# A graph layer on one core: dense units moved from the last stage to the third hop, and standard deviations picked for eight tiles at once

## What is computed

```python
def _spmm(edge_src, edge_dst, edge_weight, feats, n_nodes):
    msgs = edge_weight[:, None] * feats[edge_src]
    return jax.ops.segment_sum(msgs, edge_dst, num_segments=n_nodes)
feats = [x]
cur = x
for _ in range(n_blocks - 1):
    cur = _spmm(edge_src, edge_dst, edge_weight, cur, n_nodes)
    feats.append(cur)
concat = jnp.concatenate(feats, axis=1)
return concat @ shared_weight + output_bias
# then: x = _layernorm(x + that, axis=-1)
```

## Time and profile before

| | us |
|---|---|
| median of three runs | 1876.14 |
| lowest, highest | 1869.22, 1887.84 |
| the profiled execution | 1871.29 |
| its span, first to last instruction | 1869.5 |

### The profile page before, as it was taken

The page is one execution under the profiler, slowest core; times in us unless marked ns, Lnnn a source line. Parts: engine busy times, 40 slices in busy tenths (PEclk is TensorE's granted clock), DMA queues, the critical chain, the costliest instruction groups (busy, mean ns, idle before and its releaser), DMA issues. The chain is left out here.

```text
span 1869.5 us, 31494 instructions
## 1 busy us (share of the span) xinstructions
PE 1526.1 (82%) x7964; PEld 1254.5 (67%) x7964; DVE 1193.9 (64%) x5229; ACT 1086.5 (58%) x2674; POOL 1068.6 (57%) x1047
## 2 busy tenths in 40 slices
PE   7889888888888877488889998878877777777884
PEld 5777777777777755367768887766666656666773
DVE  6766655555556566666644445878877777777564
ACT  4665666666666643256655554656665655556565
POOL 4566666566656653656646664456555555555554
PEclk9999999999999988699989999989998888888997
DMA  8888878878778879389877776878887777777563
GB/s 253 262 262 265 268 247 260 269 252 265 253 250 267 261 232 370 107 264 310 301 232 186 187 191 208 272 239 293 270 269 256 245 242 261 242 246 249 187 206 116
DMA packets 224954, 458.74 MB, mean 245 GB/s; under 512 B 30805, under 2 KB 133144, under 8 KB 224778
## 3 DMA queue, kind: packets, MB, share of 16 engines
q1 hardware_dynamic: 174326, 349.30, 56.3%
q0 software_dynamic: 49456, 106.72, 19.7%
q10 hardware_dynamic: 996, 0.72, 0.2%
HBM read 239.08 MB, written 226.07 MB: 249 GB/s over the span
## 5 line engine op out<-in xcount | busy, mean ns | idle before, releaser
L1362 PE MATMUL ps_y<-w_sb,xT 128*128 128x256 f32 x2640 | 739.2, 409 | 92.9 <-DVE y_ring L1680 67.2
L1362 PEld LDWEIGHTS ps_y<-w_sb,xT 128*128 128x128 f32 x2640 | 502.6, 205 | 165.2 <-issue 65.5
L1680 DVE TENSOR_TENSOR y_ring<-ps_y,bias 128x512 f32<-128x512 f32 x391 | 268.9, 688 | 330.0 <-remote 161.7
L1087 ACT ACTIVATE o_ring<-y_ring,shift,rstd 128x256 f32<-128x256 f32 (+1 forms) x782 | 422.3, 590 | 0.0
L1686 DVE BATCH_NORM_STATS2 stats<-y_ring 128x6 f32<-128x256 f32 (+1 forms) x782 | 291.3, 414 | 7.4 <-remote 2.0
L827 POOL DMA_INDIRECT tails_found<-tail_keys,table_idx x200 | 201.5, 1007 | 150.5 <-issue 60.2
L827 POOL DMA_INDIRECT rows_in<-out_rows,tailx_idx x160 | 163.0, 1018 | 211.9 <-DVE sums L2329 83.0
L827 POOL DMA_INDIRECT rows_in<-in_x,gather_idx x200 | 201.2, 1006 | 128.9 <-issue 70.7
L1074 ACT COPY xT<-ps_xT 128x512 f32<-128x512 f32 x268 | 154.2, 576 | 182.7 <-remote 122.8
L831 POOL DMA_INDIRECT out_rows<-u_out,tailo_idx x197 | 200.6, 1018 | 95.5 <-issue 54.9
L1351 PE MATMUL ps_xT<-ident,x_ring 128*128 128x128 f32 x1196 | 191.7, 285 | 29.3 <-ACT xT L1074 18.6
(11 more groups left out here) (279 smaller groups left out, 2380.9 us busy)
## 6 DMA issues: line engine op xcount, KB each, us to landing
x_ring<-in_x SPq DMA_DIRECT2D x195, 512.0 KB
out_rows<-o_ring SPq DMA_DIRECT2D x195, 512.0 KB
c_rows<-zeros SPq DMA_DIRECT2D x50, 512.0 KB
c_rows<-sums SPq DMA_DIRECT2D x49, 512.0 KB
u_rows<-u_out SPq DMA_DIRECT2D x49, 512.0 KB
keys_bc<-keys_out SPq DMA_DIRECT2D x64, 256.0 KB
keys_bc<-u_rows SPq DMA_DIRECT2D x25, 512.0 KB
tails_found<-u_rows SPq DMA_DIRECT2D x12, 512.0 KB
```

What stands on the lines that cost most here:

```text
L1087: last = act.activation(o_ring[slot][0:rows, r * D:(r + 1) * D], y_ring[k][0:rows, r * D:(r + 1) * D], ACT.Identity, bias=shift[k][0:rows, ...
L1362: last = pe.matmul(ps_y[p % 2][0:rows, r * D:(r + 1) * D], columns_of(p)[0][:, q * P:q * P + rows], w_sb[:, c, :], start=c == 0, stop=c == ...
L1680: dve.tensor_tensor(y_ring[k][0:rows, half * 2 * D:(half + 1) * 2 * D], ps_y[half][0:rows, :], bias2[0:rows, :], ALU.add).then_inc(y_copie ...
```

## The change

- The ten first groups of the third hop carry two dense units each, not one. SP gets one store and one load more in each.
- The twenty kept steps of the last stage carry four and three units by turns, not four each. So ten units move from the last stage to the third hop.
- The window of deviations is 14 units wide, not 16, beginning 4 units before the tile's place, not 5.
- The three bfloat16 parts are no longer made for each step. They cover all windows, and are made in four splits (units 0 to 96 before the last stage, then 28, 24 and 14 units in steps 7, 13 and 16), in memory of buffers that are free by then.
- The one-hot matrices of partitions are made in slots 2 and 3. Column marks for all eight tiles of a step are made in one instruction in slot 5 of the step before (`mark_cols`); in slot 0 one instruction multiplies them with the spread values, in slot 1 one sums (`pick_std`, `sum_picked`).

```diff
-    D_UNIT = C_UNIT + ONE * FIRST_GROUPS + FOUR
+    D_UNIT = C_UNIT + PAIR * FIRST_GROUPS + FOUR
-    WINDOW = 16
-    WINDOW_BACK = 5
+    WINDOW = 14
+    WINDOW_BACK = 4
-    D_SIZES = (FOUR,) * KEPT_STEPS + (STEP,) * (D_STEPS - KEPT_STEPS)
+    D_SIZES = (FOUR, STEP) * (KEPT_STEPS // 2) + (STEP,) * (D_STEPS - KEPT_STEPS)
+    SPLITS = ((0, 0, 96), (7, 96, 124), (13, 124, 148), (16, 148, kept_window(KEPT_STEPS - 1)[1]))
...
-    bridge_d = (D_UNIT - FOUR, FOUR, 0, ONE)
+    bridge_d = (D_UNIT - FOUR, FOUR, 0, PAIR)
     def c_step(g):
-        return C_UNIT + ONE * g, ONE, 0, ONE if g > 0 else STEP
+        return C_UNIT + PAIR * g, PAIR, 0, PAIR if g > 0 else STEP
...
                 store_behind(c_step(g), 0)
                 if g > 0:
                     load_own(G * g + 3, 3)
+                    load_ahead(c_step(g - 1), 1)
+                store_behind(c_step(g), 1)
...
             def spread_std(d, q):
                 if q == 0:
-                    pe.wait_ge(std_chain, 6 * d + 6)
-                    until(pe, std_picked, Q * (d - 1))
+                    pe.wait_ge(parts_hot, 2 * d + 2)
+                    pe.wait_ge(std_split, 1 + 4 * splits_before(max(d - 1, 0)))
+                    until(pe, std_picked, d - 1)
...
-            def prepare_std(d, q):
+            def split_std(s, part):
+                step, first, end = SPLITS[s]
+                cols = RPP * (end - first)
+                whole = std_all[:, RPP * first:RPP * end]
+                high, mid, low = (t[:, RPP * first:RPP * end] for t in std_parts)
+                rest = std_rest[:, 0:cols]
+                if part == 0:
+                    dve.tensor_copy(high, whole).then_inc(std_split, 1)
+                if part == 1:
+                    dve.wait_ge(std_split, 4 * s + 2)
+                    dve.tensor_tensor(rest, whole, high, ALU.subtract).then_inc(std_split, 1)
+                if part == 2:
+                    dve.wait_ge(std_split, 4 * s + 3)
+                    dve.tensor_copy(mid, rest).then_inc(std_split, 1)
+                if part == 3:
+                    dve.wait_ge(std_split, 4 * s + 4)
+                    dve.tensor_tensor(low, rest, mid, ALU.subtract).then_inc(std_split, 1)
+
+            def mark_cols(d):
+                first, end = kept_window(d)
+                cols = RPP * (end - first)
+                until(dve, std_picked, d)
+                dve.tensor_tensor(col_hot[:, :, 0:cols],
+                                  window_col[:, WCOLS - cols:WCOLS].unsqueeze(1).broadcast_to([P, Q, cols]),
+                                  tail_col[:, Q * d:Q * d + Q].unsqueeze(2).broadcast_to([P, Q, cols]),
+                                  ALU.is_equal).then_inc(cols_hot, 1)
-            def pick_std(n, q, d):
-                dve.scalar_tensor_tensor(out=picked_out[q][:, 0:cols], in0=window_col[:, WCOLS - cols:WCOLS], scalar=tail_col[:, n:n + 1],
-                                         in1=ps_std[d % 2][:, WCOLS * q:WCOLS * q + cols], op0=ALU.is_equal, op1=ALU.mult,
-                                         accum_out=row_std[d % 2][:, q:q + 1]).then_inc(std_picked, 1)
+            def pick_std(d):
+                first, end = kept_window(d)
+                dve.wait_ge(std_spread, Q * d + Q)
+                dve.wait_ge(cols_hot, d + 2)
+                dve.tensor_tensor(window_view(d, picked_out), window_view(d, ps_std[d % 2][:, 0:Q * WCOLS]),
+                                  col_hot[:, :, 0:RPP * (end - first)], ALU.mult).then_inc(std_picked, 1)
+            def sum_picked(d):
+                dve.wait_ge(std_picked, d + 1)
+                dve.reduce_sum(row_std[d % 2][:, :], window_view(d, picked_out), mybir.AxisListType.X).then_inc(std_found, 1)
...
             def c_restore(n, q, d, part, turn):
-                dve.wait_ge(std_picked, n + 1)
+                dve.wait_ge(std_found, d + 3)
...
-                    if n < KEPT:
-                        pick_std(n, q, d)
+                    if n < KEPT and q < 2:
+                        (pick_std, sum_picked)[q](d)
...
-                    if d + 1 < KEPT_STEPS and q < G:
-                        prepare_std(d + 1, q)
+                    for s in range(1, len(SPLITS)):
+                        if SPLITS[s][0] == d and q < 4:
+                            split_std(s, q)
+                    if d + 1 < KEPT_STEPS and q in (2, 3):
+                        mark_parts(d + 1, q - 2)
+                    if d + 1 < KEPT_STEPS and q == 5:
+                        mark_cols(d + 1)
```

More of the change, by code:

```diff
@@ L81, in kept_window, with splits_before @@
         return max(Q * d - WINDOW_BACK, 0), Q * d - WINDOW_BACK + WINDOW
+    SPLITS = ((0, 0, 96), (7, 96, 124), (13, 124, 148), (16, 148, kept_window(KEPT_STEPS - 1)[1]))
+    def splits_before(d):
+        return sum(step <= d for step, first, end in SPLITS)
+    assert all(end <= (D_OFFS[step] - STEP if step > 0 else D_UNIT - FOUR - STEP) for step, first, end in SPLITS)
+    assert all(kept_window(d)[1] <= SPLITS[splits_before(max(d - 1, 0)) - 1][2] for d in range(KEPT_STEPS))
+    assert max(end - first for step, first, end in SPLITS) * RPP * 4 <= Q * P * 2
+    SPLIT_COLS = RPP * kept_window(KEPT_STEPS - 1)[1]
+    assert 3 * SPLIT_COLS <= Q * SLOTS
     assert all(kept_window(d)[1] <= (D_OFFS[d - 1] if d > 0 else D_UNIT - FOUR) - STEP for d in range(KEPT_STEPS))
@@ L137, in gnn_program @@
         cT = [sb(f"cT{k}", [P, 2 * D]) for k in range(2)]
-        sel = [sb(f"sel{k}", [P, P]) for k in range(G)]
+        sels = sb("sels", [P, G, P])
+        sel = [sels[:, k, :] for k in range(G)]
         keys_bc = [sb(f"keys_bc{k}", [P, Q * P]) for k in range(2)]
@@ L708, in _ @@
                 group_c(g)
-            load_ahead(c_step(FIRST_GROUPS - 1), 0)
+            for k in range(PAIR):
+                load_ahead(c_step(FIRST_GROUPS - 1), k)
             with sp.Fori(FIRST_GROUPS, n_groups) as g:
@@ new lines, in mark_parts, with window_view @@
+            def mark_parts(d, half):
+                part = 2 * (d % 2) + half
+                until(dve, std_spread, Q * (d - 1) + G * half + G)
+                dve.wait_ge(node_parts_in[part], 16 * A_STEPS + 16 * (d // 2) + 16)
+                dve.tensor_scalar(part_hot[:, half * G * P:(half + 1) * G * P], node_part_bc[part], part_number[:, 0:1], None,
+                                  ALU.is_equal).then_inc(parts_hot, 1)
+            def window_view(d, table):
+                first, end = kept_window(d)
+                return table.rearrange("p (q c) -> p q c", c=WCOLS)[:, :, 0:RPP * (end - first)]
```

59 lines of the change are left out of this document (24 added, 35 removed).

## The result

| | us |
|---|---|
| before, 20 runs beside it, median | 1869.49 |
| after, 20 runs, median | 1877.43 |
| lowest, highest of after | 1865.24, 1887.73 |
| ratio after / before | 1.0053, 95% interval 1.0027 to 1.0078 |
| the profiled execution of after, its span | 1880.17, 1878.4 |

The change made the kernel slower by half a per cent. I had forecast 6 us less; it is 8 us more, or 9.9 by the ratio. That lies inside the range and within 1%, but on the other side of zero. Repeated on two other chips, the ratio was 1.0110 (E12) and 1.0101 (E13).

A forecast was written before the change was run, and what follows sets the result against it. It took TensorE to bound the third hop, and VectorE's work plus 6.7 us of stalls a step the last stage. The sum +40 - 33 - 8 - 7 + 2 + 0 = -6 us gave 1870 us, range 1838 to 1899.

The forecast's parts named there:

- Third hop, +40: Third hop: ten groups with a second unit cost 4.0 us more each, +40 us, bounds +37 and +43.
- the hole: Third hop: product starts 0.74 us after the sum, not 0.43, awaiting ACT's copy; filling it makes a group cost 3.7 us more.
- The rival with room on TensorE: Third hop: TensorE has room, so the part costs 17 us, not 40; 1847 us in all, chance 0.08.
- Last stage, -33 for the units: Last stage: ten units fewer save VectorE's work of 3.3 us each, -33 us.
- My third rival: Last stage: three-unit steps do not shrink, saved VectorE work is waited instead; 1893 to 1911 us, said 1900, chance 0.20.
- The stalls, -8: Last stage: stalls of 6.7 us a step shrink by 0.8 us a three-unit step, -8 us, bounds 0 and -17.
- Splits, -7: Last stage: four splits in all replace four small VectorE instructions a step; -9.6 and +2.4, together -7 us.
- Picks, 0: Last stage: mark, product and sum over 448 columns take 1.6 us a step like the old picks; 0, bounds -10 to +10.
- The first split in the bridge, +2: Bridge before the last stage: longer first split of 384 columns and one mark more, where TensorE already waits, +2 us.

The follow-up runs named there:

- E12: The changed kernel, unaltered, run again on another chip against the kernel before: ratio 1.0110.
- E13: The changed kernel, unaltered, run again on a chip without late signals, against the kernel before: ratio 1.0101.
- E2: The changed kernel with the ten units put back in the last stage, new picks and splits kept, against the kernel before: ratio 0.9926.
- E14: New picks and splits alone, ten units left in the last stage, on a chip without late signals, against the kernel before: ratio 0.9915.
- E3: The kernel before, loading one tile's rows of u_rows instead of four in the kept steps, against the kernel before: ratio 1.0043.
- E4: The kernel before, with kept-row gathers bounded to one row so nearly no row is fetched, against the kernel before: ratio 1.0011.
- E5: The changed kernel with ten steps of four units, then ten of three, not by turns, against the kernel before: ratio 1.0114.
- E9: The kernel before, with half of each dense product left out in the kept steps, against the kernel before: ratio 0.9735.
- E10: The changed kernel with every dense pair's transposes issued twice in the kept steps, against the kernel before: ratio 1.0160.
- E17: The changed kernel, gathering and scattering 64 of a tile's 128 kept rows from step 1 on, against the kernel before: ratio 0.9950.

## Why the prediction was wrong, point by point

**Third hop, +40: right.** It was +36.7, just under the lower bound of 37, because the hole was filled; the last stage started 34.6 us later. The rival with room on TensorE fell. The Trainium skill (Perfetto Trace Analysis, Identifying the Most-Contended Engine) would have LDWEIGHTS time taken as the measure of fullness, and by that the part would have cost 17 us; the measurement decides for 36.7. Starts without holes were the right thing to read.

**Last stage, -33 for the units: the step that failed.** VectorE's work did fall, by 33.5 us with splits and picks, where I had 40; 26.2 of it belong to the nine units that left the stretch, 2.9 each for my 3.3. But the path did not follow: I had taken a unit's work on VectorE as its price in time. The nine units were worth 14 us in the stretch (E2 against after, E14 against E13), 1.6 each, and with what follows the ten were worth 7 to 9 us. My third rival put its point of decision at 1.6 us a unit and its price at 1893 to 1911; its mechanism, that part of what VectorE no longer does is waited instead, is what happened. On a chip with late signals the waits were those before `y_ring`; on a calm one they were ACT's for the scatters. The time stayed below that rival's because picks and splits gave 7 us more than my sum, which it shares, and the third hop cost 3 us less; and it was counted from 1876.1, which is 6.6 us above the median of before beside after.

**The stalls, -8: wrong in sign.** The waits before `y_ring` grew by 3.6 us. I leaned on "the first step of three units" as the nearest row, and I had misread it. The index copy that I took for the start of a step is made in slot 0 of the step before, so 1700.5 to 1727.4 was still a step of four. The row showed nothing about steps of three, and before has no kept step of three anywhere; the third rival's 18.5 us came from the same row. After has that step with three units: 31.5 us for 27.0, and 14.0 us of waits before `y_ring` for 6.4.

**Splits, -7: plausible, not shown by themselves.** E2's VectorE is 7.2 us below before, with the picks in it.

**Picks, 0: wrong in time.** The three instructions take 0.616, 0.609 and 0.609 us, as said. Picks and splits together gain 13.8 us (E2) and 13.4 us (E14); 7 of that stood in my sum. On the calm chip the table wait of 17 to 21 us, seen with the old picks and gone with the new, is large enough for the rest; my sum had moved the one-hot matrices without asking what their old place waited for. On the chips with late signals that wait was 0, and why the waits before `y_ring` fell by 8 us there is not shown.

**The first split in the bridge, +2: rather less.** TensorE's wait before the first spread went from 3.34 us to 3.75, and the bridge took 27.1 us for 25.6 (26.4 in E2).

**What follows the stretch** I had left at zero, without a reason. It was +3.4 us in after, +6.6 against E2, and +5.6 in E13 against E14. In the last pair 5.2 of it lie in one step, the first that computes its tiles afresh. E14's, then E13's:

```profile
1441.44:1461.08 19.64, 19.57 (x107) 17.18 (x108) 16.58 (x68) 16.41 (x41) 15.06 (x16) 1.00 0.92 322
1465.65:1490.47 24.82, 24.82 (x124) 21.09 (x123) 16.77 (x68) 18.08 (x43) 19.26 (x19) 0.90 0.83 279
```

TensorE is busy all the time in both, and in E13 it has 17 records more to do at a lower granted clock (0.90 for 1.00). In after it is the step ahead of this one that is longer, the one of 31.5 us above. No run took it apart.

**How near the number came is luck.** By the profiles, units and stalls gave 14.1 us where the sum had 41, and what follows took 3.4 where it had nothing. Against that, picks and splits gave 15.2 where it had 7, and the last stage started 34.6 us later where it had 42. The misses, +26.9, +3.4, -8.2 and -7.4, come to +14.7; three of the four were larger than the change of 6 us that I had forecast.

**What stays open.** What makes TensorE's signals late on some chips. It isn't the amount of data that E3 and E4 took away, nor the order of the steps (E5). Less work for TensorE halved the waits (E9), and it never appears in the third hop of after, where TensorE has no pause. The number of transfers on such a chip is untested.

## What to carry to other kernels

A unit of work taken out of a stage is worth what the stage's chain gives back, not its busy time: ask which transfer or signal is next in line, and look for a step of the kernel before that really has the smaller size, after checking in the code in which step its marker is issued. Move work away from a stage only where the place that it goes to costs less than that; here the stage that was full of TensorE took 3.7 us for a unit worth 1.6 where it left, and less than 0.9 once what follows was counted. The half of the change to keep is the other one: the picks alone (E2, E14) run at 0.9926 and 0.9915 of before and beat both kernels.

## What the runs showed of the hardware

- The same kernel took 1867, 1828 and 1577 us (medians) on different chips. In the last stage the difference lies in late signals: index copies 3 to 21 of after are 27.0 us apart on one chip and 21.0 on another, with nearly the same busy time of VectorE (399.11 and 397.20 us in the stretch). That is 113 of the 287 us between these two profiles; 147 lie ahead of the last stage, where no run looked, and 27 behind the stretch.
- On such chips a signal of TensorE can come 4 to 6 us after the end of its record. In the one shown the granted clock is still 1.00 when TensorE falls idle, and 0.50 when it starts again. Giving TensorE more to do raised the clock and did not shorten the stretch (E10); giving it less halved the waits (E9).
- GpSimd's indirect transfer of 64 rows took 0.96 us to issue, of 128 rows 1.03 (E17 and E13): its length hardly goes by the rows.
